# Late stage of a gated attention and FFN block: order of matrix products, statistics and maxima for the last two batches, and who computes the deviations of batch 6

## The reference

```python
n = layernorm(x); q = n @ Wq.T; k = ctx @ Wk.T; v = ctx @ Wv.T
s = where(tril, q @ k.T / 16, -inf)
p = softmax(s, axis=1)                  # over the query axis
x = x + tanh(g_xattn) * (p @ v)
m = layernorm(x)
scale = sigmoid(clip_x) * max(abs(m)) / 127     # over all 8 batches
mq = clip(round(m / scale), -128, 127) * scale  # weights are quantised likewise
h = silu(mq @ Wgate.T) * (mq @ Wup.T)           # 704 wide, quantised with a second global maximum
x = x + tanh(g_ffn) * (hq @ Wdown.T)
```

## Time and profile before

| quantity | value |
|---|---|
| median of 3 runs | 106.75 us (106.43 to 106.78) |
| profiled execution, its own time | 106.31 us |
| its span in the trace | 104.5 us |
| busy: PE, PEld, DVE, ACT, POOL | 96.9, 75.1, 80.6, 66.1, 43.6 us |
| granted TensorE clock | full speed in all 40 slices |

### The profile page before, as it was taken

How to read it: one execution, slowest core, us unless ns; L and a number is a source line. 1 busy time by engine, 2 the same in 40 slices (tenths; PEclk the granted TensorE clock), 3 DMA queues, 4 the chain that set the end, 5 groups by cost and what they waited for, 6 DMA issues and landing times.

```text
span 104.5 us, 1739 instructions
## 1 busy us (share of the span) xinstructions
PE 96.9 (93%) x562; PEld 75.1 (72%) x564; DVE 80.6 (77%) x210; ACT 66.1 (63%) x125; POOL 43.6 (42%) x78
## 2 busy tenths in 40 slices
PE   7799999999999999999999987999999697899990
PEld 2268988988889898897878975444444386889970
DVE  0544296497998999597597979559999998879991
ACT  0421071657972755636738978789888989799800
POOL 6030335047083583508517594055696560350000
PEclk9999999999999999999999999999999999999999
DMA  2999999999354010010985500000000000005555
GB/s 51 333 371 336 376 422 419 419 407 401 138 6 44 0 45 9 23 34 0 150 154 116 110 0 0 0 6 3 0 0 0 0 0 0 0 6 192 209 201 201
DMA packets 11176, 13.54 MB, mean 130 GB/s; under 512 B 6432, under 2 KB 7712, under 8 KB 11168
## 3 DMA queue, kind: packets, MB, share of 16 engines
q1 hardware_dynamic: 10304, 12.39, 37.9%
q10 hardware_dynamic: 864, 1.05, 3.2%
HBM read 10.09 MB, written 2.10 MB: 117 GB/s over the span
## 4 chain that ended last, share of the span: by engine, by line
PE 47%; DVE 20%; DMA 16%; POOL 5%; issue 4%; ACT 3%; SPq 1%; DVEq 0%; POOLq 0%
PE ps L465 9%; DVE hmax L1100 9%; PE ps L686 9%; DMA spread<-rstd 8%; PE ps L503 5%; PE ps L485 5%; DMA r_wide<-spread 5%; DMA wk_sb<-in_wk 4%; DVE shared L1095 4%; PE ps L635 2%; POOL shared L436 2%; PE ps L523 2%; PE ps L540 2%; PE ps L691 2%; PE ps L516 2%
## 5 line engine op out<-in xcount | busy, mean ns | idle before, releaser
L635 PE MATMUL ps<-xq,wguT 128*128 128x512 bf16 x78 | 17.2, 379 | 0.7 <-DVE xq L1075 0.6
L436 POOL TENSOR_TENSOR shared<-up_sb,silu 128x1024 f32<-128x1024 f32 x5 | 11.8, 2366 | 9.5 <-ACT up_sb L830 9.5
L635 PEld LDWEIGHTS ps<-xq,wguT 128*128 128x128 bf16 x80 | 7.8, 98 | 9.8 <-issue 0.6
L465 PE MATMUL ps<-wvT,shared 128*128 128x256 f32 x56 | 13.3, 381 | 0.0
L485 PE MATMUL ps<-shared,a_sb 128*128 128x256 f32 x56 | 13.2, 379 | 0.0
L1100 DVE TENSOR_REDUCE hmax<-shared 128x1 f32<-128x2048 f32 (+1 forms) x6 | 12.7, 2109 | 0.6
L825 ACT ACTIVATE silu<-ps,gu_scale 128x1024 f32<-128x1024 f32 x10 | 11.2, 1115 | 2.1 <-PE ps L635 2.1
L503 PEld LDWEIGHTS ps<-uT,shared 128*128 128x128 f32 x64 | 10.7, 190 | 2.2 <-DVE uT L892 1.0
L503 PE MATMUL ps<-uT,shared 128*128 128x256 f32 (+1 forms) x64 | 12.0, 330 | 0.2 <-DVE uT L892 0.2
L465 PEld LDWEIGHTS ps<-wvT,shared 128*128 128x128 f32 x56 | 10.6, 190 | 1.8 <-DMA shared<-in_xc 0.4
L686 PE MATMUL ps<-hq,wdT 128*128 128x256 bf16 x80 | 10.6, 273 | 0.3 <-DVE hq L1135 0.3
(11 more groups left out here) (120 smaller groups left out, 188.4 us busy)
## 6 DMA issues: line engine op xcount, KB each, us to landing
shared<-in_xc SPq DMA_DIRECT2D x6, 512.0 KB, 10.8
out<-xn SPq DMA_DIRECT2D x7, 256.0 KB, 2.0
xs<-in_x SPq DMA_DIRECT2D x3, 512.0 KB, 8.4
shared<-in_wgu SPq DMA_DIRECT2D x3, 512.0 KB, 7.8
wd<-in_wd SPq DMA_DIRECT2D x1, 896.0 KB, 11.8
shared<-in_xc SPq DMA_DIRECT2D x3, 256.0 KB, 6.9
xs<-in_x ACTq DMA_DIRECT2D x2, 256.0 KB, 5.4
r_wide<-spread SPq DMA_DIRECT2D x4, 128.0 KB, 4.7
```

The lines of the kernel that those rows point to most:

```text
L436: nc.gpsimd.tensor_tensor(hid[:, 2 * i + 1, :], up_sb[i % 2][:], silu1[i % 2][:], ALU.mult).then_inc(hid_done[1], 1)
L465: last = nc.tensor.matmul(values_bank(b, k), ctxT(b)[:, e, k * P:(k + 1) * P], weights[:, e, :], start=(e == 0), stop=(e == KT - 1))
L635: last = nc.tensor.matmul(bank(4 * half + 2 * g + c), wguT[:, i, g, k, :], xq[:, k, col:col + CH], start=(k == 0), stop=(k == KT - 1))
```

## The change

For the last two batches it reorders work on all engines, and moves some of it from one to another.

- SyncE: the factors of batch 7 are written to DRAM before those of batch 6 are read back. Each batch has a semaphore of its own.
- TensorE: `attend(5)` goes ahead of `project_queries(7)`, `attend(6)` ahead of `scores(7)`, and the four transposes of batch 0 ahead of the last attention products.
- VectorE: `residual(5)`, `invert_sum(6)` and `stats2(5)` go ahead of the scaling of the queries of 7; `residual(6)` ahead of `row_max(7)`; `stats2(6)` and `variance2(6)` ahead of the two reciprocals of 7; the maximum of the deviations of 6 ahead of the statistics of 7.
- GpSimd computes `neg_dev` of batch 6 (a negated mean, then two column-scaled operations) in place of ScalarE, before both inverse deviations. It casts half of the down weights; ScalarE the other half, after the values of 6.

```diff
@@ -328,20 +330,31 @@
             load_xc(6)
             load_xc(7)
 
-            for b in range(WIDE_FROM, B):
+            def deviation_to_dram(b):
                 n = b - WIDE_FROM
                 sp.wait_ge(rstd1_done, b + 1)
-                sp.dma_start(spread[n], rstd1[:, b]).then_inc(spread_out, 16)
-                sp.wait_ge(spread_out, 16 * (n + 1))
+                sp.dma_start(spread[n], rstd1[:, b]).then_inc(spread_out[n], 16)
+
+            def deviation_to_all(b):
+                n = b - WIDE_FROM
+                sp.wait_ge(spread_out[n], 16)
                 everywhere = spread[n].rearrange("p t -> (p t)").unsqueeze(0).to_broadcast([P, P * QT])
                 sp.dma_start(r_wide[:, n].rearrange("q p t -> q (p t)"), everywhere).then_inc(r_wide_here[n], 16)
+
+            for b in range(WIDE_FROM, LAST - 1):
+                deviation_to_dram(b)
+                deviation_to_all(b)
+            deviation_to_dram(LAST - 1)
+            deviation_to_dram(LAST)
+            deviation_to_all(LAST - 1)
+            deviation_to_all(LAST)
 
             for s in range(SLOTS):
                 sp.wait_ge(wgu_q_done, s + 1)
                 sp.dma_start_transpose(wguT[:, s].rearrange("p n k i -> p (n k) i"),
                                        wgu_q[:, s].rearrange("p n d -> p (n d)")).then_inc(wguT_here, 16)
-            sp.wait_ge(wd_q_done, 1)
             for t in range(KT):
+                sp.wait_ge(wd_q_done[t], 1)
                 sp.dma_start_transpose(wdT[:, :, t * P:(t + 1) * P], wd_q[:, t]).then_inc(wdT_here, 16)
 
             for c in range(STEPS - 1):
...
@@ -412,11 +426,22 @@
                     inverse_deviation1(b + 3)
                 if b == 3:
                     inverse_deviation1(LAST)
+            pool.wait_ge(mv2_done, LAST)
+            nc.gpsimd.tensor_scalar(neg_mean[:, LAST - 1], mv2[:, LAST - 1, :, 0], -1.0, 1.0, ALU.mult,
+                                    ALU.mult).then_inc(neg_mean_done, 1)
+            pool.wait_ge(neg_mean_done, LAST)
+            pool.wait_ge(factors_set, 2)
+            for t in range(QT):
+                nc.gpsimd.tensor_scalar(neg_dev[:, t, :], xs[:, NT - 2 * QT + t, :], neg_mean[:, LAST - 1, t:t + 1],
+                                        minus_one[:, 0:1], ALU.add, ALU.mult).then_inc(neg_dev6_done, 1)
             for b in (LAST - 1, LAST):
                 inverse_deviation2(b)
             for b in (LAST - 1, LAST):
                 pool.wait_ge(rstd2_done, b + 1)
-                pool.wait_ge(neg_dev_done, QT * (b - LAST + 2))
+                if b == LAST - 1:
+                    pool.wait_ge(neg_dev6_done, QT)
+                else:
+                    pool.wait_ge(neg_dev_done, QT)
                 for t in range(QT):
                     last = nc.gpsimd.tensor_scalar(xn2[:, QT * b + t, :], neg_dev[:, QT * (b - LAST + 1) + t, :],
                                                    inverse2(b)[:, t:t + 1], -1.0, ALU.mult, ALU.mult)
...
@@ -578,15 +603,16 @@
 
             p = LAST % 2
             scores(LAST - 1)
+            attend(LAST - 2)
             project_queries(LAST)
-            attend(LAST - 2)
+            attend(LAST - 1)
             scores(LAST)
-            attend(LAST - 1)
             values_tile(LAST, 1).then_inc(v_done, 1)
             pe.wait_ge(rbc_ready, WIDE_FROM)
             nc.tensor.matmul(bank(RB)[:, 0:D], ident[:], xs[:, NT - 2, :], start=True, stop=False)
             pe.wait_ge(max_done, B + 1)
             nc.tensor.matmul(bank(SC)[:, 0:D], ident[:], xs[:, NT - 1, :], start=True, stop=False)
+            transposes2(0)
             pe.wait_ge(exp_done, B)
             pe.wait_ge(vh_ready, QT * LAST + 1)
             nc.tensor.matmul(bank(RB)[:, 0:D], probs0[p][:, 0:P], vh[p][:, 0, :], start=False, stop=True).then_inc(
...
@@ -596,7 +622,7 @@
             pe.wait_ge(vh_ready, QT * LAST + 2)
             nc.tensor.matmul(bank(SC)[:, 0:D], probs1[p][:], vh[p][:, 1, :], start=False, stop=True).then_inc(
                 attn_done, 1)
-            for b in (0, 1, 2, 4, 5):
+            for b in (1, 2, 4, 5):
                 transposes2(b)
             pe.wait_ge(x1_done, LAST)
             keep_warm(WARM_BEFORE_MAX, AT)
...
@@ -786,18 +812,15 @@
                     quantise_down_weights(0)
                 if b == 1:
                     quantise_weights(2)
-                if b == 5:
-                    quantise_down_weights(1)
             exponentials(LAST - 1)
             values_out(LAST - 1)
+            quantise_down_weights(1)
+            act.wait_ge(wdint_done, KT)
+            nc.scalar.copy(wd_q[:, 1], wd_i16[:, 1]).then_inc(wd_q_done[1], 1)
 
             exponentials(LAST)
             values_out(LAST)
             nc.scalar.activation(silu0[:, 0:1], scalars[:, 0:1], ACT.Silu).then_inc(silu_loaded, 1)
-            act.wait_ge(mv2_done, LAST)
-            for t in range(QT):
-                nc.scalar.activation(neg_dev[:, t, :], xs[:, NT - 2 * QT + t, :], ACT.Identity,
-                                     bias=mv2[:, LAST - 1, t, 0:1], scale=-1.0).then_inc(neg_dev_done, 1)
             for t, bk in enumerate((RB, SC)):
                 act.wait_ge(mv2_done, LAST + t + 1)
                 nc.scalar.activation(neg_dev[:, QT + t, :], bank(bk)[:, 0:D], ACT.Identity, bias=mv2[:, LAST, t, 0:1],
...
@@ -1026,29 +1049,34 @@
 
             row_max(LAST - 1)
             largest2(LAST - 3)
+            residual(LAST - 2)
+            invert_sum(LAST - 1)
+            stats2(LAST - 2)
             scale_queries_whole(LAST)
-            invert_sum(LAST - 1)
-            residual(LAST - 2)
-            stats2(LAST - 2)
             variance2(LAST - 2)
+            residual(LAST - 1)
             row_max(LAST)
+            stats2(LAST - 1)
+            variance2(LAST - 1)
             for k in range(QT):
                 dve.wait_ge(exp_done, B + k)
                 nc.vector.reciprocal(inv_sum[:, LAST, k:k + 1], row_sum[:, LAST, k:k + 1]).then_inc(inv_sum_done, 1)
-            residual(LAST - 1)
-            stats2(LAST - 1)
-            variance2(LAST - 1)
             largest2(LAST - 2)
 
+            def largest_deviation(n0, n1):
+                nc.vector.tensor_reduce(xmax[:, B - 2 + n0:B - 2 + n1], neg_dev[:, n0:n1, :], AX.X, ALU.max,
+                                        apply_absolute_value=True).then_inc(xmax_done, n1 - n0)
+
+            dve.wait_ge(neg_dev6_done, QT)
+            largest_deviation(0, QT)
             for t, bk in enumerate((RB, SC)):
                 dve.wait_ge(attn_done, B + t)
                 nc.vector.bn_stats(bn2[:, LAST, t, :], bank(bk)[:, 0:D]).then_inc(bn2_done, 1)
                 dve.wait_ge(bn2_done, B + t)
                 nc.vector.bn_aggr(mv2[:, LAST, t, :], bn2[:, LAST, t, :]).then_inc(mv2_done, 1)
-            for n0, n1 in ((0, QT), (QT, QT + 1), (QT + 1, 2 * QT)):
-                dve.wait_ge(neg_dev_done, n1)
-                nc.vector.tensor_reduce(xmax[:, B - 2 + n0:B - 2 + n1], neg_dev[:, n0:n1, :], AX.X, ALU.max,
-                                        apply_absolute_value=True).then_inc(xmax_done, n1 - n0)
+            for t in range(QT):
+                dve.wait_ge(neg_dev_done, t + 1)
+                largest_deviation(QT + t, QT + t + 1)
             dve.wait_ge(xmax_done, B - 2 + 2 * QT)
             dve.wait_ge(rstd2_done, B)
             nc.vector.tensor_tensor_reduce(xmax_all[:], xmax[:], xfactor[:], 1.0, 0.0, ALU.mult, ALU.max,
```

More of the change, by code:

```diff
@@ L87, in gated_block @@
         minus_half = sb("minus_half", [P, QT])
+        minus_one = sb("minus_one", [P, 1])
         bnq = sb("bnq", [P, KT, 6])
@@ L225, in gated_block @@
         rbc_ready = sem("rbc_ready")
-        spread_out = sem("spread_out")
+        spread_out = [sem(f"spread_out{b}") for b in range(WIDE_FROM, B)]
         r_wide_here = [sem(f"r_wide_here{b}") for b in range(WIDE_FROM, B)]
@@ L258, in gated_block @@
         wdint_done = sem("wdint_done")
-        wd_q_done = sem("wd_q_done")
+        wd_q_done = [sem(f"wd_q_done{t}") for t in range(KT)]
+        neg_dev6_done = sem("neg_dev6_done")
         wguT_here = sem("wguT_here")
@@ L369, in _ @@
             nc.gpsimd.tensor_copy(ident_bf[:], ident[:]).then_inc(consts, 1)
+            nc.gpsimd.memset(minus_one[:], -1.0).then_inc(factors_set, 1)
             nc.gpsimd.memset(xfactor[:], 1.0).then_inc(factors_set, 1)
@@ L384, in inverse_deviation2 @@
                 if b == LAST - 1:
-                    pool.wait_ge(factors_set, 1)
+                    pool.wait_ge(factors_set, 2)
                 nc.gpsimd.tensor_tensor(inverse2(b), var2[:, b], minus_half[:], ALU.pow).then_inc(rstd2_done, 1)
@@ L405, in _ @@
                 if b == LAST - 1:
-                    pool.wait_ge(wdint_done, KT)
-                    nc.gpsimd.tensor_copy(wd_q[:], wd_i16[:]).then_inc(wd_q_done, 1)
+                    pool.wait_ge(wdint_done, 1)
+                    nc.gpsimd.tensor_copy(wd_q[:, 0], wd_i16[:, 0]).then_inc(wd_q_done[0], 1)
```

## The result

The changed kernel took 107.15 us (median of 9 runs, 106.89 to 107.63), the kernel before in the same measurement 106.51 (9 runs). The ratio is 1.0071, with a 95% interval of 1.0054 to 1.0088: slower by 0.6 to 0.9 us. The forecast was slower, at +0.4 us. (The ratio is worked out over executions no more than 1.5% above the fastest of their kernel; the two medians alone give 1.0060.)

A forecast was written before the change was run, and what follows sets the result against it. It took VectorE's tail, as late as TensorE's, to decide the barrier. Late reciprocals, GpSimd's deviations and the tail put L1054 at 61.21 against 60.79: +0.42 us, on the median's scale 106.75 + 0.4 = 107.15; range 106.5 to 107.6.

The forecast's parts named there:

- The +0.42 of the sum: At the barrier: L1054 starts at 61.21 us against 60.79, so everything behind it comes 0.42 us later.
- The transfer's wait: TensorE ahead of the scores of 7: 0.49 us lost to late factors; written early they land near 47.0, wait gone.
- The order: TensorE's new order: scores of 7 end at 54.98, 0.81 us later than the 54.17 of before.
- Late reciprocals: VectorE, behind the statistics of 6: reciprocals of 7 late by 0.44 us, stalling TensorE before the last attention product.
- GpSimd's pair: Two column-scaled operations for the deviations of 6 on GpSimd: 1.10 us, taken from L394.
- the lower bound from L421: GpSimd's two operations on the deviations of 6 at 0.46 us each, 0.93 for both, as with a constant.
- The second case: Rival, no change: GpSimd's pair ends early, VectorE reduces batch 6 before attention delivers; 106.9 to 107.0, chance 0.27.
- one reduction beside it doesn't slow GpSimd: VectorE's reduction beside GpSimd's pair never contends, leaving +0.42; the rival, GpSimd blocked, gave +1.07, 107.8, chance 0.08.
- A wrong bound: Statistics of 7 on VectorE: attention alone would have allowed them to end at 59.81, against 60.07 forecast.
- ScalarE's path: Tail: second deviation of 7 ends at 60.63, its reduction at 61.1, just ahead of L1054 at 61.21 set by GpSimd.
- The casts: Down-weight casts costed at nothing: ScalarE has over 2 us between the values of 6 and the exponentials of 7.

The follow-up runs named there:

- a_recip: The changed kernel with the two reciprocals of 7 put back ahead of the statistics of 6: 107.98 us, 1.0153 of the kernel before.
- a_oldsp: The changed kernel with SyncE's old order (6 read back before 7 is written): 107.06 us, 1.0063 of the kernel before.
- a_const: The changed kernel with a constant -1 in GpSimd's two operations on the deviations of 6, replacing a column: 106.88 us, 1.0057 of the kernel before.
- a_turn_late: The changed kernel with the transposes of batch 0 put back behind the last attention products: 107.26 us, 1.0063 of the kernel before.
- a_redlate: The changed kernel with the maximum of the deviations of 6 behind the statistics of 7, as before: 106.94 us, 1.0043 of the kernel before.
- b_sp: The kernel before with only SyncE's new order, factors of 7 written ahead of the read-back of 6: 106.26 us, 1.0000 of the kernel before.
- b_half: The kernel before with the last maximum of normalised rows (batch 5) reading one of two row tiles: 106.83 us, 1.0015 of the kernel before.

## Why the prediction was right, point by point

- **Side and size.** Forecast +0.4, measured 0.6 to 0.9 in time: the side is right, the size a quarter to a half too small. That the median is the forecast 107.15 to the digit is luck: the forecast started from 106.75, and the kernel before took 106.51 beside the changed one, a difference of 0.64. In the profile it was +0.55 to L1054's start and +0.45 to the scale. The +0.42 of the sum was made for L1054's start, and there it was 0.13 short: 0.06 because L1082 began 0.14 behind GpSimd, where I had 0.08, and 0.07 that had come together before the statistics of 7, at the scores of 7 (0.03), the reduction of GpSimd's deviations and the handoffs.
- **What was missing** lies behind the barrier. I took everything there to follow L1054 unchanged. From the scale to the start of the last VectorE instruction it took 101.72 - 61.71 = 40.01 before and 102.70 - 62.59 = 40.11 in the changed kernel. The chain that ended last shows the place, the first two casts of quantised rows on VectorE, with TensorE's first product of the gate and up weights right behind them. Before, and in the changed kernel:

```profile
63.56 0.50 DVE xq L1075 x2
```

```profile
64.44 0.58 DVE xq L1103 x2
```

  GpSimd writes the rows of 6 and 7 later relative to the scale, and its own share of the quantising comes behind them. Before, and in the changed kernel:

```profile
62.39 1.12 POOL L427 TENSOR_SCALAR xq_i<-xn2T,act_inv 128x1024 int16<-128x1024 f32 x1
```

```profile
63.55 1.11 POOL L452 TENSOR_SCALAR xq_i<-xn2T,act_inv 128x1024 int16<-128x1024 f32 x1
```

  Before, GpSimd ended at 63.51 and the first cast started at 63.56 and took 0.28; now GpSimd ended at 64.66, behind the start of the first cast at 64.44, which took 0.37. So it is in all the profiles: in the five where GpSimd's share reached into the first cast (changed, a_recip, a_oldsp, a_const, a_turn_late) the way from the scale to the last VectorE instruction was 40.09 to 40.12, in the nine others 40.00 to 40.02. a_redlate, where GpSimd ended 0.05 ahead of the cast, has 40.01. That GpSimd slows the cast is read from this; no run was made for it. The other 0.12 of the "rest" lies behind the last VectorE instruction (2.78 before, 2.90 now), where kernels with the same end differ by as much (2.71 to 2.90). Sum by the profile: 0.45 + 0.10 = 0.55 us, just below the interval of the time (0.58 to 0.94); what is beyond it isn't shown.
- **The transfer's wait** is gone as said: the read-back of 7 was issued at 42.70 and took 3.9 us, so the factors were there at 46.6, where I had 47.0. Its price of 0.49 us was wrong as a gain: alone it is worth 0.1 (b_sp). I had read TensorE's wait and not seen that the row maxima at 54.41 started behind a variance that ended at 54.50, on a VectorE without idle time. In the sum this did no harm, because the row maxima of 7 were placed by TensorE's new order.
- **The order:** scores of 7 placed 0.81 later; measured, from the mark, 0.84 at TensorE's next product (55.44 - 47.61 = 7.83 against 54.17 - 47.18 = 6.99) and 8.03 - 7.23 = 0.80 at the row maxima. Right.
- **Late reciprocals:** 0.44 forecast, (9.54 - 8.03) - 1.07 = 0.44 measured. Right, and TensorE's gap stands where it was said, 0.38 long behind 0.44 of transposes (0.22 in the brackets, behind their recorded 0.60), forecast some 0.4.
- **GpSimd's pair:** 1.10 taken, 1.09 measured; the lower bound from L421 holds for the form with a constant (0.92, a_const). The second case needed the earlier pair and was not met. That one reduction beside it doesn't slow GpSimd agrees with the rule cited from the Trainium skill (SBUF — State Buffer, Who interferes with whom), though the two overlapped for a third of a microsecond only (57.61 to 57.92).
- **A wrong bound:** I let the statistics of 7 wait for L594, to 59.81. The code gives the first tile's signal at L592 and the second's at L597. a_redlate shows the floor 0.37 under the changed kernel's, not 0.26. GpSimd's wait covered the error. For the same reason the 0.17 from 58.06 to 58.23 was no handoff: in the kernel before, the statistics of the first tile stood behind VectorE's own reduction (57.66).
- **ScalarE's path** was forecast 0.1 ahead of GpSimd's in the tail. In the changed kernel the reductions ended at 60.58 + 0.95 = 61.53 and the inverse deviation at 61.63: right.
- **The casts** cost nothing, as said: ScalarE's cast ended at 53.98 + 0.94 = 54.92, and ScalarE then stood idle for 1.18 us ahead of the exponentials of 7.

## What to carry to other kernels

A wait on the engine that the chain names is worth its length only if the engine that works next has idle time right ahead of the handoff; read that one's row there. Where work is moved forward on two engines, add up the idle time of the third between two fixed points. Here VectorE had 1.91 us of it before (1.23 + 0.46 + 0.22) and 2.42 after (0.06 + 0.25 + 0.43 + 0.56 + 0.88 + 0.24), from the row maxima of 6 to the start of L1054 or L1082. The difference of 0.51 is nearly the whole loss between these points, 0.55. A small gain was to put a short instruction into an idle gap (variance behind the row maxima), not to move a whole product.

## What the runs showed of the hardware

- A column operand costs GpSimd 0.17 us over two operations of 128x256 (1.09 against 0.92).
- The same 8-byte-per-partition write to DRAM took 5.60 us where it was issued 0.36 us behind a read-back (41.20, 41.56), and 2.68 and 3.2 where it was issued 2.8 and 3.1 us behind one (batches 6 and 5, in the kernel before). The wait that follows from it differs between executions: in the profile of b_half the scaling of 7 came 0.17 us later after the mark than in the first profile of the same order. Written early, the factors were in time in every profile.
- A cast of 128x512 from int16 to bf16 on VectorE took 0.28 us where GpSimd's `tensor_scalar` of 128x1024 had ended, and 0.37 where that was still running at its start (before, changed). GpSimd's small one behind it (128x12), which ran beside a cast in both, left that at 0.28.
- Profiles of kernels that are alike up to there reach the scaling of 6 anywhere from 47.08 to 47.99 us, largely because of the first loads: the first of TensorE's small transposes of the inverse deviations already starts anywhere from 8.94 to 9.76. A comparison of two profiles of a small change needs a common mark behind them.
